# A two-layer graph network on one core: how the first layer forms and adds its messages' parts

## The chip, the core and the metric

The program runs on one of the eight cores of a Trainium2 chip. The metric is the device time of one execution in microseconds (us). The engines are named as in the profile: PE is TensorE (PEld is its weight load), DVE is VectorE, ACT is ScalarE, POOL is GpSimd and SP is SyncE.

## What is computed

There are 6250 nodes with 128 features and 100000 edges, sorted by their target `dst`. All is float32. The first layer is, with a layer norm behind it:

```python
msg_input = jnp.concatenate([h[src], h[dst], edge_feat], axis=-1)
messages = jax.nn.silu(msg_input @ W1 + b1) @ W2 + b2
agg = jax.ops.segment_sum(messages, dst, num_segments=h.shape[0])
upd_in = jnp.concatenate([h, agg], axis=-1)
h_new = jax.nn.silu(upd_in @ W3 + b3) @ W4 + b4
return h_new + h
```

The second layer sums `h[src]` by target, applies two small matrices, a layer norm and a relu. The change touches only the first layer.

## The kernel before

The edges stand in 196 groups of 512 (`GE`), four edges on each of 128 partitions (`CH` = 4). Two groups make a pair, so there are 98 pairs (`NPAIR`), and the targets of a group lie in a window of 64 nodes (`W`).

**The table of source terms.** `h @ W1[:128] + b1` is computed once for all nodes and stored in the tensor src_term. For each group POOL issues four indirect DMAs (line 873), each of which brings one row for each of 128 edges into `gath`, a ring of eight slots, so POOL may be four pairs ahead. The first two pairs (`FROM_X`) gather rows of x itself instead. A group's gather waits until the slot's last content, eight groups before, was used. Before, that is the counter `pre_ps`.

**The pair's work.** DVE makes the window's target one-hots in `terms_l` (line 1923), one pass of 64 partitions for each half of the pair, which also counts the edges of each node into `deg_col`. ACT copies the turned edge features and the window's target terms four times over (lines 1013 and 1014). In `pre_sums` PE multiplies them, four products of 128 rows a half (line 1233), adds the gathered rows by a product with the identity (line 1240), and counts `pre_ps` up. ACT applies silu into `msg` (line 1022). In `message_sums` PE sums messages by target with the one-hots `oh` (line 1250) and the degrees (line 1252). DVE adds these sums to `S` and `T` (`add_sums`, lines 1934 to 1938).

**The order.** Each engine runs turns (`steps`), and the list of stages at its end gives for each stage a lag: stage (lag, body) does pair s - lag in turn s. Each engine does the stages of a turn in the order of the list and waits in order. On DVE a turn is: unit rows of the node update (`rows0`, every second turn), `windows` of pair s-1, `one_hots` of s-2, `add_sums` of s-3, then `sort_edges`. `sort_edges` is a bitonic sort of the first half's edges by source, which the second layer uses; it fills turns 5 to 42 in portions. After turn 45 `early_hots` takes its place: one-hots for sums of the second layer that are made ahead. On PE a turn is `turn_ef` of s-1, `pre_sums` of s-2, `early_sums` and `early_rows`, `message_sums` of s-3, then the node update of a tile every second turn.

**After the pairs.** POOL issues 16 more gathers for two bridge blocks and then computes the last tile's inverse root (line 918). The rows of the first layer must all be stored before the second layer begins (line 1993 on DVE, line 1421 on PE).

## Time and profile before

| | us |
|---|---|
| median of the three runs | 1933.41 |
| lowest and highest run | 1929.03, 1937.31 |
| span of the profiled execution, first to last instruction | 1500.6 |
| its own time beside the span | not recorded; the timed median lies 432.8 above the span |
| busy of PE, PEld, DVE, ACT, POOL | 1285.9, 1063.6, 1014.5, 642.1, 1107.0 |

A row of a timeline is: start, duration, engine, line, operation, written<-read tiles, shapes, and in brackets how long the engine was idle before it and what ended that. DMA-issuing instructions are not counted as busy on other queues, and a matmul's duration overlaps the next one's, so that the pace of products is read from start to start.

### The profile page before, as it was taken

To read this page: it belongs to the slowest core of one execution; us is meant where nothing else is said; L and a number is where in the kernel's file an instruction comes from. 1 tells how busy PE (TensorE), PEld (TensorE's weight loads), DVE (VectorE), ACT (ScalarE), POOL (GpSimd) and SP (SyncE) were. 2 spreads that over 40 slices of the span, in tenths; PEclk is the share of its full clock that TensorE was granted. 3 is DMA by queue.
4 is the path that set the end of the run, shared out by engine and by line. 5 is a ranking of instruction groups with operands and counts; after the bars stand their busy time and mean duration, and the time that the engine had idled before them with its cause. 6 is when DMAs were issued, how large, how long until landed. Compare 5 with 4: busy or idle time off the path is not lost.

```text
span 1500.6 us, 31339 instructions
## 1 busy us (share of the span) xinstructions
PE 1285.9 (86%) x8165; PEld 1063.6 (71%) x8165; DVE 1014.5 (68%) x2310; ACT 642.1 (43%) x1257; POOL 1107.0 (74%) x1164
## 2 busy tenths in 40 slices
PE   6788789778777889888888888885999999999992
PEld 6666667556556667767767776764899999998982
DVE  4678888677665565665566656643666888878866
ACT  2744556555555555555556555551111111111111
POOL 5777777777777777777777777777777777777771
PEclk9898889999998999999999999997999999999996
DMA  6533333333336454454455445433887778778731
GB/s 206 135 85 92 93 95 94 95 96 91 95 90 119 118 138 125 126 136 131 125 131 133 125 128 135 113 80 105 258 261 230 208 230 241 222 230 241 213 92 47
DMA packets 189124, 214.15 MB, mean 143 GB/s; under 512 B 60426, under 2 KB 149517, under 8 KB 189011
## 3 DMA queue, kind: packets, MB, share of 16 engines
q1 hardware_dynamic: 138399, 131.62, 28.9%
q0 software_dynamic: 36352, 74.52, 21.3%
q10 hardware_dynamic: 14260, 6.68, 1.6%
q8 instruction: 49, 0.80, 0.2%
q14 instruction: 64, 0.52, 0.1%
HBM read 202.74 MB, written 9.85 MB: 142 GB/s over the span
## 4 chain that ended last, share of the span: by engine, by line
POOL 42%; PE 32%; issue 15%; DVE 4%; DMA 4%; SPq 1%; ACT 1%; DVEq 0%; ACTq 0%; POOLq 0%
POOL gath L873 42%; PE bank L1434 9%; PE bank L1410 8%; PE bank L1362 4%; DMA gath<-src_term,src_col 2%; PE bank L1240 2%; PE bank L1250 2%; PE bank L1233 2%; PE bank L1421 1%; DMA T<-in_x 1%; DMA gath<-layer_input,src_col 1%; PE bank L1396 1%; PE bank L1383 1%; PE bank L1441 0%; PE bank L1456 0%
## 5 line engine op out<-in xcount | busy, mean ns | idle before, releaser
L873 POOL DMA_INDIRECT gath<-src_term,src_col x768 | 737.2, 960 | 234.2 <-issue 230.2
L873 POOL DMA_INDIRECT gath<-layer_input,src_col x336 | 329.6, 981 | 105.6 <-issue 100.6
L1240 PE MATMUL bank<-gath,ident 128*128 128x512 f32 x384 | 218.3, 652 | 114.5 <-DMA gath<-src_term,src_col 113.8
L1233 PEld LDWEIGHTS bank<-terms_r,terms_l 128*128 128x128 f32 x1568 | 209.4, 201 | 83.1 <-issue 69.2
L1233 PE MATMUL bank<-terms_r,terms_l 128*128 128x128 f32 x1568 | 219.6, 286 | 30.4 <-ACT msg L1022 22.0
L1923 DVE TENSOR_SCALAR_CACHE_REDUCE terms_l<-dst_bc,node_col 64x512 f32<-64x512 int32 x196 | 221.0, 1128 | 13.1 <-issue 7.2
L1250 PEld LDWEIGHTS bank<-oh,msg 128*128 128x128 f32 x1568 | 198.7, 202 | 26.9 <-issue 26.1
L1934 DVE TENSOR_TENSOR S<-S,bank 128x128 f32 x98 | 28.1, 286 | 270.2 <-PE bank L1252 178.2
L1250 PE MATMUL bank<-oh,msg 128*128 128x128 f32 x1568 | 202.3, 285 | 0.0
L1434 PE MATMUL bank<-S 128*128 128x288 f32 x672 | 170.0, 406 | 0.1
L1649 DVE TENSOR_TENSOR oh<-bank,dst_rel 128x1024 f32<-128x1024 f32 x140 | 169.8, 1213 | 0.0
L1240 PEld LDWEIGHTS bank<-gath,ident 128*128 128x128 f32 x384 | 61.2, 201 | 129.7 <-DMA gath<-src_term,src_col 129.4
L1434 PEld LDWEIGHTS bank<-S 128*128 128x128 f32 x672 | 124.5, 190 | 31.1 <-issue 0.2
L1022 ACT ACTIVATE msg<-bank 128x512 f32<-128x512 f32 x196 | 115.8, 599 | 59.8 <-PE bank L1240 57.4
L1013 ACT COPY terms_l<-bank 64x512 f32<-64x512 f32 x196 | 113.7, 580 | 40.0 <-PE bank L1203 28.6
L1076 ACT COPY S<-bank 128x512 f32<-128x512 f32 x84 | 49.2, 586 | 185.8 <-PE bank L1410 181.8
L1993 DVE TENSOR_TENSOR S<-bank,dst_of 128x2304 f32<-128x2304 f32 x44 | 112.0, 2548 | 10.1 <-PE bank L1434 3.8
L1014 ACT COPY terms_r<-bank 64x512 f32<-64x512 f32 x196 | 113.4, 578 | 0.0
L1035 ACT ACT_TABLE_LOAD x48 | 61.6, 1283 | 66.9 <-DVE mv L2025 66.4
L1362 PE MATMUL bank<-oh,gath 128*128 128x128 f32 x672 | 84.4, 279 | 5.1 <-DMA gath<-layer_input,src_col 5.1
L1362 PEld LDWEIGHTS bank<-oh,gath 128*128 128x128 f32 x672 | 80.4, 195 | 5.7 <-DMA gath<-layer_input,src_col 5.7
L1987 DVE TENSOR_SCALAR xT<-xT,even_odd 128x1024 f32<-128x1024 f32 x84 | 60.5, 762 | 5.4 <-DMA xT<-sorted_src 5.4
(219 smaller groups left out, 1754.7 us busy)
## 6 DMA issues: line engine op xcount, KB each, us to landing
dst_bc<-in_dst SPq DMA_DIRECT2D x195, 128.0 KB
xT<-sorted_src SPq DMA_DIRECT2D x42, 512.0 KB
xs<-layer_input SPq DMA_DIRECT2D x136, 128.0 KB
gath<-src_term,src_col POOLq DMA_INDIRECT x768
terms_l<-layer_input SPq DMA_DIRECT2D x88, 128.0 KB
terms_r<-layer_input SPq DMA_DIRECT2D x88, 128.0 KB
msg<-layer_input SPq DMA_DIRECT2D x80, 128.0 KB
ef_s<-in_edge_attr SPq DMA_DIRECT2D x97, 64.0 KB
```

Source lines behind the costliest of these rows:

```text
L873: g.indirect_dma_start(out=to[:, j * D:(j + 1) * D], out_offset=None, in_=table[0:rows, :], in_offset=bass.IndirectOffsetOnAxis(ap=indices ...
L1013: a.copy(terms_l[r, u, h, :, :], bank[4][r, 0:P].unsqueeze(1).to_broadcast([W, CH, P]))
L1014: last = a.copy(terms_r[r, u, 1 - h, :, :], bank[4][r, P:2 * P].unsqueeze(1).to_broadcast([W, CH, P]))
L1022: a.activation(msg[:, 2 * (m % 2) + h, :], bank[h][:, :], ACT.Silu).then_inc(msg_made, 1)
L1233: mm(bank[h][:, j * D:(j + 1) * D], terms_l[:, u, h, j, :], terms_r[:, u, h, j, :], start=j == 0, stop=False)
L1240: mm(bank[h][:, :], ident[:, :], gath[:, slot, :], start=False, stop=True).then_inc(pre_ps, 1)
L1250: mm(bank[2 + u][:, 0:PW], msg[:, 2 * u + c // CH, c % CH * D:(c % CH + 1) * D], oh[:, u, c, :], start=c == 0, stop=c == 2 * CH - 1)
L1362: last = mm(bank[2 + u][:, 0:PW], gath[:, s, c % CH * D:(c % CH + 1) * D], oh[:, u, c, :], start=c == 0, stop=c == 2 * CH - 1)
L1410: last = mm(bank[h][:, c * D:(c + 1) * D], src_hot[:, u, w, e], x_near[m][h * CH + c][:, w, :], start=w == 0, stop=w == 1)
L1434: last = mm(bank[4][:, 0:DW], rows_kept[:, c // CH, c % CH * D:(c % CH + 1) * D], dst_hot[:, u, c, :], start=o % LATE == 0 and c == 0, sto ...
L1649: ve_.tensor_tensor(oh[:, u, :, :], iota_ps.unsqueeze(1).to_broadcast(shape), dst_rel[:, ds((k + first) * (2 * CH), 2 * CH)].unsqueeze(2). ...
L1923: ve_.tensor_scalar(terms_l[r, u, h, :, :], dst_bc[r, u, :].rearrange("n (p j) -> n j p", j=CH), node_col[r, ds(k, 1)], None, ALU.is_equal ...
```

## The change

The operands of the first layer's products are laid out anew, and the gathered rows are added elsewhere.

- `windows`: one DVE pass of 128 partitions makes both one-hots (`dst_is`), without counting. ACT counts in a new stage `degrees`, a copy of 128x512 with a sum.
- `edge_features`: one ACT copy of 128x256 to `ef_b` in place of four of 64x512. The edge weights `wef_of` are a constant.
- `pre_sums`: for each half one 64-row product of 512 columns, then four 64-row products of 128 columns each, the halves in turn. The identity product is gone. Half h of pair k waits for `rows_added` of half h of pair k-1, since both use bank h.
- `add_rows`: a new last stage of DVE's turn, pair s-2. It waits for PE's bank and for the gathered rows and writes their sum to `msg`. ACT's silu works on `msg` in place. The ring's slot is free once `rows_added` counts.

```diff
@@ load_pair (SP)
-                sp.wait_ge(ohT_made, done(2 * k - 3))
+                sp.wait_ge(ohT_made, done(k - 2))
@@ gather_sources (POOL)
                     if g >= RING:
-                        pool.wait_ge(pre_ps, done(g - RING))
+                        pool.wait_ge(rows_added, done(g - RING))
@@ edge_features, degrees, messages (ACT)
-                for h in range(2):
-                    r = slice(h * W, (h + 1) * W)
-                    a.copy(terms_l[r, u, h, :, :], bank[4][r, 0:P].unsqueeze(1).to_broadcast([W, CH, P]))
-                    last = a.copy(terms_r[r, u, 1 - h, :, :], bank[4][r, P:2 * P].unsqueeze(1).to_broadcast([W, CH, P]))
-                last.then_inc(efT_made, 1)
+                a.copy(ef_b[:, u, :], bank[4][:, 0:2 * P]).then_inc(efT_made, 1)
+
+            def degrees(k, m, q):
+                act.wait_ge(ohT_made, done(k))
+                act.wait_ge(sums_ps, done(k - DEEP))
+                act.wait_ge(deg_made, done(k - 1))
+                a.activation(pre[:, :].rearrange("p (j e) -> p j e", j=CH), dst_is[:, m % 2, :, :], ACT.Copy,
+                             accum_out=deg_col[:, m:m + 1]).then_inc(deg_made, 1)
...
-                    act.wait_ge(pre_ps, done(g))
-                    act.wait_ge(sums_ps, done(k - 2))
-                    a.activation(msg[:, 2 * (m % 2) + h, :], bank[h][:, :],
-                                 ACT.Silu).then_inc(msg_made, 1)
+                    act.wait_ge(rows_added, done(2 * k + h))
+                    of = msg[:, 2 * (m % 2) + h, :]
+                    a.activation(of, of, ACT.Silu).then_inc(msg_made, 1)
@@ pre_sums (PE)
+                for h in range(2):
+                    pe.wait_ge(rows_added, done(2 * k + h - 2))
+                    mm(bank[h][:, :], ef_b[own[h], u, 0:P], wef_of[own[h], :], start=True, stop=False)
+                for j in range(CH):
+                    for h in range(2):
+                        last = j == CH - 1 and not from_rows
+                        made = mm(bank[h][:, j * D:(j + 1) * D], dst_is[own[h], u, j, :], ef_b[own[h], u, P:2 * P],
+                                  start=False, stop=last)
+                        if last:
+                            made.then_inc(pre_ps, 1)
@@ windows, add_rows (DVE)
+                dve.wait_ge(deg_made, done(k - 2))
+                ve_.tensor_scalar(dst_is[:, u, :, :], dst_bc[:, u, :].rearrange("n (p j) -> n j p", j=CH),
+                                  node_col[:, ds(k, 1)], None, ALU.is_equal).then_inc(ohT_made, 1)
+
+            def add_rows(k, m, q):
+
+                u = m % 2
+                dve.wait_ge(sums_ps, done(k - 2))
                 for h in range(2):
...
+                    slot = 2 * m + h
+                    to = msg[:, 2 * u + h, :]
+                    dve.wait_ge(pre_ps, done(2 * k + h))
...
+                    dve.wait_ge(gathered[slot], 16 * CH * (q + 1))
+                    ve_.tensor_tensor(to, bank[h][:, :], gath[:, slot, :], ALU.add).then_inc(rows_added, 1)
@@ the stage lists (ACT, DVE)
-                  of_pair(1, edge_features), of_pair(0, window_x),
+                  of_pair(1, edge_features), of_pair(0, window_x), of_pair(2, degrees),
...
-                  of_early(1, early_hots))
+                  of_early(1, early_hots), of_pair(2, add_rows))
```

The order of DVE's instructions around the end of turn 5, before: from the sums' addition (`S`) past the last exchange of the sort portion to the next turn's windows. The sort portion between is left out.

```order
L1934 ISA [waits sums_added,sums_ps,zeroed]
L1934 TENSOR_TENSOR S<-S,bank 128x128
L1744 TENSOR_TENSOR src_rows_f<-src_rows_f,bank 112x64x2x2 [waits sort_steps]
L1923 TENSOR_SCALAR terms_l,deg_col<-dst_bc,node_col 64x512 [waits sums_ps,pre_ps,dst_bc_in1]
L1923 TENSOR_SCALAR terms_l,deg_col<-dst_bc,node_col 64x512
L1649 TENSOR_TENSOR oh<-bank,dst_rel 128x1024 [waits sums_ps]
```

The same place now. `dst_rows_f` and `src_rows_f` are the sort's keys.

```order
L1949 ISA [waits sums_added,sums_ps,zeroed]
L1949 TENSOR_TENSOR S<-S,bank 128x128
L1748 TENSOR_TENSOR src_rows_f<-src_rows_f,bank 112x32x2x4 [waits sort_steps]
L1940 TENSOR_TENSOR msg<-bank,gath 128x512 [waits gathered_0,pre_ps,sums_ps]
L1940 TENSOR_TENSOR msg<-bank,gath 128x512 [waits gathered_1,pre_ps]
L1925 TENSOR_SCALAR terms<-dst_bc,node_col 128x512 [waits deg_made,pre_ps,dst_bc_in0]
L1653 TENSOR_TENSOR oh<-bank,dst_rel 128x1024 [waits sums_ps]
```

The two additions into `msg` stand behind the sort portion and ahead of the next turn's windows, and wait for gathers, for PE and for the pair before the last.

PE's order for one pair before (from `pre_sums` of pair 3 to `message_sums` of pair 2).

```order
L1233 MATMUL bank<-terms_r,terms_l 128x128 [waits msg_made,ohT_made,efT_made]
L1233 MATMUL bank<-terms_r,terms_l 128x128 x3
L1240 MATMUL bank<-gath,ident 128x512 [waits gathered_6]
L1233 MATMUL bank<-terms_r,terms_l 128x128 [waits msg_made]
L1233 MATMUL bank<-terms_r,terms_l 128x128 x3
L1240 MATMUL bank<-gath,ident 128x512 [waits gathered_7]
L1250 MATMUL bank<-oh,msg 128x128 [waits msg_made,sums_added,oh_made]
L1250 MATMUL bank<-oh,msg 128x128 x3
L1250 MATMUL bank<-oh,msg 128x128 [waits msg_made]
L1250 MATMUL bank<-oh,msg 128x128 x3
```

And now, where `terms` holds `dst_is`, `ef_b` and `wef_of`.

```order
L1234 MATMUL bank<-terms 128x512 [waits rows_added,ohT_made,efT_made]
L1234 MATMUL bank<-terms 128x512 [waits rows_added]
L1238 MATMUL bank<-terms 128x128 x8
L1254 MATMUL bank<-oh,msg 128x128 [waits msg_made,sums_added,oh_made]
L1254 MATMUL bank<-oh,msg 128x128 x3
L1254 MATMUL bank<-oh,msg 128x128 [waits msg_made]
L1254 MATMUL bank<-oh,msg 128x128 x3
L1257 MATMUL bank<-ident,deg_col 1x128 [waits deg_made]
```

The waits for gathers left PE. In their place the second product of 512 columns waits for DVE's addition for the pair before, and the message sums of that pair still stand behind it.

## Rows read from the trace of the kernel before

**Rows 1.** The page: span, and the chain that ended last by engine.
```profile
span 1500.6 us, 31339 instructions
...
POOL 42%; PE 32%; issue 15%; DVE 4%; DMA 4%; SPq 1%; ACT 1%; DVEq 0%; ACTq 0%; POOLq 0%
```

**Rows 2.** POOL: the group of gathers, and its last work ahead of layer two.
```profile
L873 POOL DMA_INDIRECT gath<-src_term,src_col x768 | 737.2, 960 | 234.2 <-issue 230.2
...
1034.72 0.25 POOL L918 TENSOR_SCALAR var_eps<-mv 128x2 f32<-128x2 f32 x1
```

**Rows 3.** Windows: busy time by engine, PEclk (granted clock), DMA share, GB/s.
```profile
115.00:125.00 10.00, 6.61 (x30) 4.83 (x29) 7.57 (x25) 7.20 (x13) 7.63 (x8) 0.71 0.38 101
150.00:300.00 150.00, 122.38 (x722) 94.64 (x721) 117.86 (x297) 86.44 (x168) 113.95 (x119) 0.91 0.37 94
300.00:450.00 150.00, 118.02 (x691) 89.68 (x690) 103.78 (x256) 82.35 (x158) 113.77 (x119) 0.92 0.37 93
600.00:750.00 150.00, 132.56 (x858) 105.36 (x857) 92.67 (x215) 84.80 (x172) 114.02 (x119) 1.00 0.49 129
```

**Rows 4.** Timeline of DVE: end of turn 5, then turn 6.
```profile
90.32 0.42 DVE L1744 TENSOR_TENSOR src_rows_f<-src_rows_f,bank 112x256 f32<-112x256 f32 x1
94.14 0.27 DVE L1934 TENSOR_TENSOR S<-S,bank 128x128 f32 x1
...
94.81 0.41 DVE L1736 COPY bank<-src_rows_f 112x256 f32<-112x256 f32 x1
...
98.64 0.42 DVE L1744 TENSOR_TENSOR src_rows_f<-src_rows_f,bank 112x256 f32<-112x256 f32 x1
```

**Rows 5.** Timeline of PE after an idle stretch, and one pair later.
```profile
120.73 2.04 PE L1233 MATMUL bank<-terms_r,terms_l 128*128 128x128 f32 x8 [3.39 <-ACT msg L1022]
122.56 1.91 PE L1240 MATMUL bank<-gath,ident 128*128 128x512 f32 x2
...
125.98 1.07 PE L1240 MATMUL bank<-gath,ident 128*128 128x512 f32 x2
126.88 1.95 PE L1250 MATMUL bank<-oh,msg 128*128 128x128 f32 x16
128.76 0.38 PE L1252 MATMUL bank<-ident,deg_col 128*1 128x128 f32 x2
...
132.16 1.05 PE L1233 MATMUL bank<-terms_r,terms_l 128*128 128x128 f32 x8
133.05 1.02 PE L1240 MATMUL bank<-gath,ident 128*128 128x512 f32 x2
```

**Rows 6.** Groups of DVE instructions between 10 and 60 us, shapes kept apart.
```profile
L1545 DVE TENSOR_TENSOR T<-bank,b_bc 128x512 f32<-128x512 f32 x12 | 8.3, 688 | 12.9 <-PE bank L1160 7.6 <-DMA b_bc<-in_L_gnn_b 5.3
L1923 DVE TENSOR_SCALAR_CACHE_REDUCE terms_l<-dst_bc,node_col 64x512 f32<-64x512 int32 x5 | 5.6, 1130 | 2.3 <-issue 2.2
```

**Rows 7.** Timeline of a turn with early work of the second layer.
```profile
709.44 0.62 DVE L1987 TENSOR_SCALAR xTs<-As,even_odd 128x256 f32<-128x256 f32 x2
...
709.83 1.05 POOL L873 DMA_INDIRECT gath<-src_term,src_col  x1 [0.30 <-issue]
...
709.97 0.75 DVE L1993 TENSOR_TENSOR src_rows_f<-bank,dst_of 128x576 f32<-128x576 f32 x1
...
714.61 1.13 PE L1396 MATMUL bank<-dst_rows_f,As 128*128 128x288 f32 x4
...
715.58 1.05 PE L1383 MATMUL bank<-xs,xTs 128*128 128x128 f32 x8
```

**Rows 8.** Timeline of the first layer's end.
```profile
1016.11 1.29 PE L1240 MATMUL bank<-gath,ident 128*128 128x512 f32 x2 [3.17 <-DMA gath<-src_term,src_col]
...
1024.50 0.29 DVE L1934 TENSOR_TENSOR S<-S,bank 128x128 f32 x1 [2.60 <-PE bank L1252]
...
1031.98 0.25 DVE L2025 BATCH_NORM_AGGREGATE mv<-st 128x2 f32<-128x6 f32 x2
...
1039.10 5.02 DVE L1993 TENSOR_TENSOR S<-bank,dst_of 128x2304 f32<-128x2304 f32 x2 [2.67 <-DMA layer_input<-ot]
```

More of the change, by code:

```diff
@@ L897, in gather_bridge @@
                     g = 2 * k + h
-                    pool.wait_ge(pre_ps, done(g - RING))
+                    pool.wait_ge(rows_added, done(g - RING))
                     gather_rows(x1_d, EARLY_TILES * P, g % RING, bridge_rows[:, k - NPAIR, h * CH:(h + 1) * CH],
@@ L1110, in any_messages @@
                 act.wait_ge(any_pre_ps, done(i - 1))
[L1111 removed]
+                a.copy(ef_b[0:W, 0, 0:P], bank[4][0:W, 0:P]).then_inc(any_efT_made, 1)
                 act.wait_ge(any_pre_made, done(i))
@@ L1227, in pre_sums @@
                 pe.wait_ge(efT_made, done(k))
-                pe.wait_ge(ohT_made, done(2 * k + 1))
+                pe.wait_ge(ohT_made, done(k))
+                from_rows = isinstance(k, int) and k < FROM_X
+                own = [slice(h * W, (h + 1) * W) for h in range(2)]
                 for h in range(2):
-                    g = 2 * k + h
-                    pe.wait_ge(msg_made, done(g - 2))
-                    for j in range(CH):
-                        mm(bank[h][:, j * D:(j + 1) * D], terms_l[:, u, h, j, :], terms_r[:, u, h, j, :],
-                           start=j == 0, stop=False)
-                    if isinstance(k, int) and k < FROM_X:
-                        add_from_x(g, bank[h])
-                        continue
-                    slot = 2 * m + h
-                    pe.wait_ge(gathered[slot], 16 * CH * (q + 1))
-                    mm(bank[h][:, :], ident[:, :], gath[:, slot, :], start=False, stop=True).then_inc(pre_ps, 1)
+                    pe.wait_ge(rows_added, done(2 * k + h - 2))
[7 more added lines that the diff above has]
+                            made.then_inc(pre_ps, 1)
+                if from_rows:
+                    for h in range(2):
+                        add_from_x(2 * k + h, bank[h])
             def message_sums(k, m, q):
```

109 lines of the change are left out of this document (52 added, 57 removed).

## The prediction

> **What bounds the kernel now.** First the page: the chain that ended last gives 42% of the span to POOL and 15% to issue, which in the first layer is the gap between two gathers [rows 1]. The group of gathers says what a gather costs: 960 ns busy and 234.2/768 = 0.30 us idle, put down to issue and not to another engine [rows 2]. So one gather takes 1.26 us, the eight of a pair 10.1 us, and 98 pairs about 991 us. In the windows POOL is busy 114 of 150 us in every stage of the first layer, which is 119 gathers of 1.26: POOL never stops [rows 3]. PE, DVE and ACT are fitted under it. DVE is the next: 117.9 of 150 us between 150 and 300 us, where the sort runs, against 92.7 of 150 after it [rows 3]. At the end POOL counts once more: after the last pair's rows come 16 bridge gathers, and then the last inverse root at 1034.72; the second layer begins at 1039.10 [rows 2, 8]. From there PE is the bound, and the change does not touch that part.
>
> So what PE, DVE or ACT save inside the first layer is worth nothing as long as POOL is fed. What the change can do is to let the engines behind POOL fall back. The question is one turn of DVE: is it longer than 10.1 us?
>
> **The change part by part.** *DVE's own work.* Two passes of 1130 ns and their counts go [rows 6], 2.3 us. One pass of 128x512 comes, for which I have no row of the same form: it lies between the two-column-value pass of 128x256 (0.31 us each, two in 0.62 [rows 7]), doubled in size, 0.5 us, and the old pass, 1.13 us. I take 0.8 (either way it lies beside PE's work and is not on the path below). Two additions of 128x512 from PSUM come, priced at the 688 ns of the nearest form [rows 6], 1.3 us in start to start. In sum DVE does a little less than before.
>
> *ACT.* Four copies become one, and a counting copy comes. ACT was far from its limit, the counts have a turn's time until PE asks for them, so this is priced at nothing; if it were on the path it would cost one 0.6 us copy a pair.
>
> *PE.* Per pair two groups of identity products go, 0.86 us each from start to start (125.98 to 126.88 holds 0.90) [rows 5]. Two products of 512 columns come, with 64 rows, at the same price. Eight products of 128 columns stay, 0.89 us for four (132.16 to 133.05) [rows 5], now of 64 rows with the halves in turn. No row shows two halves of the array at work together: the bounds are 1.8 us a pair, as now, and half of it, 0.9. I take the middle, 1.35.
>
> *SP, POOL.* SP's loads wait for the same pass as before, POOL's gathers for `rows_added` eight groups back instead of `pre_ps`: nothing as long as the lag stays under some 28 us (three pairs less the landing).
>
> *The new ring of waits.* This is the cost. Call E(k) the time at which DVE ends the second addition of pair k. Behind it come, each waiting for the one before: PE's second 512-column product of pair k+1 (it needs bank 1), its small products, the message sums of pair k, DVE's addition of these sums, DVE's sort portion, and only then the additions of pair k+1, for DVE works in order and the additions stand last in its turn. Behind a waiting addition stand DVE's next windows, its one-hots and the next sort portion, and PE and ACT wait for these. Before, no addition stood there: DVE sorted while PE worked on the pair.
>
> At PE's higher clock the turn is: 1.1 (the rest of the first wide product, which started 0.65 us before E, and the second) + 1.35 small + 1.9 message sums (126.88 to 128.76) + 0.3 degrees + 0.2 until DVE starts [rows 5] = 4.8. Then 0.7 for the sums (94.14 to 94.81), the sort portion 4.2 (94.81 to 99.06; the portions of turns 6 to 19 are alike but for one of 3.2), and 1.3 for the additions [rows 4, 6]. Sum 11.0 us, with 10.6 and 11.5 for the two prices of the small products. That is already over 10.1.
>
> But then PE, with some 7 us of work a turn, is idle for about 4 us in each. What such an idle does is in the trace: after 3.39 us of idle the same four products take 1.8 us from start to start and not 0.89, and this lasts from 120.73 to 125.98, 5.3 us [rows 5]; the granted clock of that window is 0.71, a part at 1.2 GHz and the rest at 2.4 [rows 3]. So I reckon PE's part anew with the first 5.3 us at the lower level: wide products 1.7 each, of which E comes 0.65 into the first, so E+2.8; small ones 1.8 to 2.7, so E+4.6 to 5.5; sums and degrees at the higher level again, 2.2, and 0.2: E+7.0 to 7.9, middle 7.4. With 0.7, 4.2 and 1.3 the turn takes **13.6 us** (13.2 to 14.1). It leaves PE idle for some 4 us again, so it repeats itself.
>
> *The sum along E.* In the kernel before the sort portion of turn 5 ends at 90.74 [rows 4]. Now turn 5 ends with E(3), and turns 3 to 5 already wait for additions and for PE behind them: some 4 us more, and 1.3 for the additions themselves, E(3) = 96. Turns 6 to 19: 14 x 13.6 = 190. Turns 20 to 44 have portions from 0.4 to 5.4 us; DVE is busy 103.8 of 150 us there [rows 3], the long portions lose what the short ones win, and I take 25 x 10.2 = 255. Turns 45 to 93 carry the early work. There PE has 1.86 us more between the small products and the message sums (714.61 to 715.58, and 0.89 for the next eight instructions), DVE 1.3 in place of the sort (709.44 to 710.72) [rows 7]: 4.8 + 1.9 + 0.7 + 1.3 + 1.3 = 10.0, at the higher clock, since PE is idle under 2 us of it and PEclk is 1.00 in that stage already [rows 3]. 49 x 10.0 = 490. The last six turns have neither, 4.8 + 0.7 + 1.3 and unit rows, 7.8 each: 47. E(97) = 96 + 190 + 255 + 490 + 47 = 1078. Then 0.6 silu, half the message sums, degrees and DVE's start, 3.3 in all, and from the sums' addition to the second layer what it was, 1039.10 - 1024.50 = 14.6, less the 2.5 us for which DVE's mv at 1032.2 waited for POOL at 1034.72: 12.1 [rows 8, 2]. The second layer begins at 1078 + 3.3 + 12.1 = 1094 in place of 1039: **+55 us**, and the span is 1555. The profile's span is 1500.6, the median of the runs 1933.41, and I carry the 432.8 between them over unchanged: **1988 us**. This case's own range: with 13.2, 9.6 (small products overlapping) and a slower end bound by POOL +37, with 14.1 and 10.5 throughout +95, so 1970 to 2028.
>
> **Rules beside the rows.** Of overlapping halves no row here shows anything. The Trainium skill (TensorEngine Tiling (Array Packing), Tiling Modes) has two row tiles of 64 work in parallel, and a change of tiling mode drain the array. By the first the turns would take 13.2 and 9.6 us and the whole +37, by the second more than I took; the sum above goes by the middle.
>
> **The rivals.** *POOL still paces (0.17).* If PE's part behind E is shorter than I think, or the clock stays up with halves overlapping, the turn of 10.6 us falls back 0.5 us in each of 14, the ring takes it up, and it is regained in the short turns. Then POOL's 10.1 us a pair set the time, as its unbroken row says [rows 2, 3]: 1933, with at most 5 us either way. *The ring binds at the higher clock (0.19).* Turns of 11.0 to 11.5 us and E(3) = 96: E(17) = 96 + 157 = 253, 46 behind the gathers, of which 28 are free, so POOL is held up for 15 to 20 us: 1950. [...]
>
> *DVE's pass holds up the gathers (0.06).* The gather that runs beside the pair of passes at 709.44 takes 1.05 us and not 0.96 [rows 7]. If the new pass, a form without a count, does the same, each pair costs POOL 0.1 us, up to 0.3 for a pass of twice the length: 98 x 0.1 to 0.3 = 10 to 29 us, 1943 to 1962. The Trainium skill (GPSIMD Engine Reference, Specifications) says that GpSimd shares its SBUF interfaces with VectorE, which contend when VectorE is in a 2-port mode; by that rule, the trace agrees. Where DVE's ring already binds, this is hidden.
>
> *The other side: the last turns get shorter (0.05).* Message sums of pair 96 no longer stand behind the last pair's gather. From that landing at 1016.1 to 1024.5 there are 8.4 us [rows 8], now about 0.65 + 3.3: 4.4 less. POOL's inverse root caps that at 2.5 us unless it comes earlier; with PE kept at its higher clock into the second layer it could be some 9 to 10 us, 1923. This decides only if no turn is over 10.1 us.
>
> The forecast has 0.53. A measurement tells from no change what is over 0.5%, 9.7 us. Slower by more: 0.53 + 0.19 + 0.04 of the pass = 0.76; within: 0.17 + 0.02 = 0.19; faster: 0.05. The range goes from 1932, in the middle of the case in which POOL paces, to 2030.
>
> **What would show it.** Right: POOL's gathers waiting for DVE's L1940 from about 95 us on; DVE idle ahead of the sums' addition in each sort turn by some 4 us, released by PE's degrees product; PE idle ahead of its 512-column product, released by DVE's addition; PEclk between 0.7 and 0.85 from 100 to 250 us; a turn of 13 to 14 us there and 10 later; the second layer starting near 1094 and unchanged in length. Wrong: POOL busy 114 of 150 us throughout, small products at 0.45 us for eight instructions, or a sort turn under 10.5 us. The forecast errs most in the clock, which doubles PE's part, and in turns 45 to 93, where 0.5 us a turn is 25 us.

## The result, and the profile after

| us | before | after |
|---|---|---|
| median of four runs | 1931.72 | 2185.73 |
| lowest and highest | 1929.03, 1937.31 | 2179.06, 2188.75 |
| span of the profiled execution | 1500.6 | 2177.2 |

The changed kernel takes 1.1288 times as long, interval 1.1248 to 1.1328. That is 254 us more, where I had forecast 55. Its profiled execution took 2179.06 us, 1.9 more than its span, so here a trace shows the whole of what is timed. The page of the changed kernel, against [rows 1, 2]:

```profile
span 2177.2 us, 31275 instructions
...
PE 1402.9 (64%) x8173; PEld 1148.2 (53%) x8173; DVE 973.7 (45%) x2212; ACT 526.7 (24%) x1159; POOL 1104.5 (51%) x1161
...
L874 POOL DMA_INDIRECT gath<-src_term,src_col x768 | 741.0, 965 | 739.2 <-DVE msg L1940 514.9
...
L1949 DVE TENSOR_TENSOR S<-S,bank 128x128 f32 x98 | 28.3, 289 | 768.4 <-remote 416.6
...
L1925 DVE TENSOR_SCALAR terms<-dst_bc,node_col 128x512 f32<-128x512 int32 x98 | 66.9, 683 | 6.7 <-issue 6.7
```

A gather still takes 965 ns, but the idle time in front of the 768 has gone from 234.2 to 739.2 us, and 514.9 of it ends with DVE's addition (line 1940). DVE itself waits 768.4 us in front of its addition of the message sums (line 1949). DVE and ACT are less busy than in the profile of before, POOL as busy, and PE is 117 us busier (1402.9 against 1285.9) at a mean granted clock of 0.778 against 0.945. The rest of the added time is waits. Windows of the changed kernel, columns as in [rows 3]:

```profile
150.00:300.00 150.00, 70.99 (x407) 60.85 (x407) 69.57 (x194) 37.21 (x83) 69.17 (x72) 0.70 0.21 55
...
900.00:1050.00 150.00, 100.32 (x557) 73.49 (x558) 56.94 (x131) 43.59 (x103) 74.50 (x78) 0.73 0.32 86
1200.00:1350.00 150.00, 103.67 (x574) 76.23 (x572) 56.25 (x131) 44.60 (x101) 76.68 (x79) 0.73 0.34 87
```

72 gathers in 150 us are 16.7 us a pair, 79 are 15.2, against 10.1 before [rows 3]. PEclk is low in the last two stages as well, where I had put PE at its higher clock. The additions give E(k) as I called it. DVE's rows of the changed kernel at E(3) (the second of the two ends 0.6 us later), E(17), E(42), E(91) and E(97):

```profile
120.76 0.68 DVE L1940 TENSOR_TENSOR msg<-bank,gath 128x512 f32<-128x512 f32 x1
...
358.26 1.28 DVE L1940 TENSOR_TENSOR msg<-bank,gath 128x512 f32<-128x512 f32 x2
...
744.29 1.29 DVE L1940 TENSOR_TENSOR msg<-bank,gath 128x512 f32<-128x512 f32 x2
...
1486.18 1.27 DVE L1940 TENSOR_TENSOR msg<-bank,gath 128x512 f32<-128x512 f32 x2
...
1560.60 1.29 DVE L1940 TENSOR_TENSOR msg<-bank,gath 128x512 f32<-128x512 f32 x2
```

| step | forecast us | measured us |
|---|---|---|
| E(3) | 96 | 122.0 |
| turns 6 to 19 | 14 x 13.6 = 190 | 14 x 17.0 = 237.5 |
| turns 20 to 44 | 25 x 10.2 = 255 | 25 x 15.4 = 386.0 |
| turns 45 to 93 | 49 x 10.0 = 490 | 49 x 15.1 = 741.9 |
| last six | 47 | 74.4 |
| E(97) | 1078 | 1561.9 |
| E(97) to the second layer | 15.4 | 15.0 |

So every turn is some 3.4 to 5.2 us over my sum. But the kernel before has as much that its one profile did not show, and that has to come first.

### The profile page after: what moved, and what is told of

The parts are those of the page before. It is cut to its first block, busy times and chain, and to the rows that moved or that the text cites. A ratio compares the mean times of both kernels' runs of the same rounds, so it can differ in the third digit from the quotient of the medians.

```text
span 2177.2 us, 31275 instructions
## 1 busy us (share of the span) xinstructions
PE 1402.9 (64%) x8173; PEld 1148.2 (53%) x8173; DVE 973.7 (45%) x2212; ACT 526.7 (24%) x1159; POOL 1104.5 (51%) x1161
## 3 DMA queue, kind: packets, MB, share of 16 engines
HBM read 202.74 MB, written 9.85 MB: 98 GB/s over the span
## 4 chain that ended last, share of the span: by engine, by line
another core or an unknown queue 49%; issue 13%; DVE 12%; SPq 10%; PE 9%; DVEq 3%; ACT 2%; DMA 1%; ACTq 0%; POOLq 0%; POOL 0%
PE bank L1439 3%; DVEq L1944 2%; SPq L719 2%; SPq L781 2%; PE bank L1415 2%; SPq L784 2%; DVE msg L1940 1%; DVE bank L1740 1%; DVE src_rows_f L1744 1%; DVE oh L1653 1%; SPq L733 1%; SPq L792 1%; ACT S L1077 1%; DVE src_rows_f L1748 1%
## 5 line engine op out<-in xcount | busy, mean ns | idle before, releaser
L874 POOL DMA_INDIRECT gath<-src_term,src_col x768 | 741.0, 965 | 739.2 <-DVE msg L1940 514.9
L1234 PE MATMUL bank<-terms 64*128 64x512 f32 x392 | 225.0, 1120 | 344.3 <-DVE msg L1940 341.1
L1949 DVE TENSOR_TENSOR S<-S,bank 128x128 f32 x98 | 28.3, 289 | 768.4 <-remote 416.6
L1024 ACT ACTIVATE msg<-msg 128x512 f32<-128x512 f32 x196 | 122.0, 630 | 953.9 <-DVE msg L1940 925.8
L1234 PEld LDWEIGHTS bank<-terms 64*128 64x128 f32 x392 | 71.6, 305 | 367.8 <-issue 287.2
L1254 PE MATMUL bank<-oh,msg 128*128 128x128 f32 x1568 | 223.2, 289 | 56.0 <-issue 54.5
L1238 PEld LDWEIGHTS bank<-terms 64*128 64x128 f32 x1568 | 219.6, 315 | 61.9 <-issue 61.3
L1439 PE MATMUL bank<-S 128*128 128x288 f32 x672 | 192.9, 444 | 34.9 <-ACT S L1077 30.3
L1238 PE MATMUL bank<-terms 64*128 64x128 f32 x1568 | 198.3, 396 | 0.0
L1202 PE MATMUL bank<-ident,ef_s 128*128 128x128 f32 x98 | 37.5, 382 | 175.0 <-ACT As L1069 132.5
L1367 PE MATMUL bank<-oh,gath 128*128 128x128 f32 x672 | 103.4, 288 | 59.2 <-issue 58.0
L1940 DVE TENSOR_TENSOR msg<-bank,gath 128x512 f32<-128x512 f32 x192 | 122.9, 681 | 0.9 <-DVE dst_rows_f L1748 0.5
L1925 DVE TENSOR_SCALAR terms<-dst_bc,node_col 128x512 f32<-128x512 int32 x98 | 66.9, 683 | 6.7 <-issue 6.7
```

The source lines that it names most:

```text
L874: g.indirect_dma_start(out=to[:, j * D:(j + 1) * D], out_offset=None, in_=table[0:rows, :], in_offset=bass.IndirectOffsetOnAxis(ap=indices ...
L1024: a.activation(of, of, ACT.Silu).then_inc(msg_made, 1)
L1234: mm(bank[h][:, :], ef_b[own[h], u, 0:P], wef_of[own[h], :], start=True, stop=False)
L1238: made = mm(bank[h][:, j * D:(j + 1) * D], dst_is[own[h], u, j, :], ef_b[own[h], u, P:2 * P], start=False, stop=last)
L1254: mm(bank[2 + u][:, 0:PW], msg[:, 2 * u + c // CH, c % CH * D:(c % CH + 1) * D], oh[:, u, c, :], start=c == 0, stop=c == 2 * CH - 1)
L1367: last = mm(bank[2 + u][:, 0:PW], gath[:, s, c % CH * D:(c % CH + 1) * D], oh[:, u, c, :], start=c == 0, stop=c == 2 * CH - 1)
```

## The kernel before, profiled again

The kernel before without a change, once more.

> The kernel before, unchanged, once more. The profiled span of the kernel before was 1500.6 us while its timed executions took 1932, and that of the changed kernel was 2177 against 2186. Theory A (the one profiled execution of the kernel before was unlike its timed ones, and the timed ones wait longer after each semaphore): a profile of a span near 1925, POOL idle for more than 0.30 us ahead of many gathers, and an addition of the sums that starts 1 to 3 us after PE's degrees product. Theory B (430 us lie outside the span): span 1500 again, time 1932.

Measured: 1893.91 us against 1897.55 for the runs of before beside it, ratio 0.9985 (0.9953 to 1.0016). Its profiled execution took 1891.83 us with a span of 1889.9. So theory A came true, though DVE's addition starts later still than it said. The 432.8 us do not lie outside the span: the first profile was of an execution unlike the timed ones. Windows of its two layers, for the first profile (1500.6), this one and the changed kernel, in this order:

```profile
0.00:1039.10 1039.10, 858.62 (x5297) 678.93 (x5297) 666.13 (x1614) 568.23 (x1097) 777.45 (x828) 0.94 0.44 115
1039.10:1500.00 460.90, 427.23 (x2868) 384.68 (x2868) 348.38 (x696) 73.90 (x160) 329.57 (x336) 0.96 0.70 206
```
```profile
0.00:1297.80 1297.80, 975.21 (x5297) 750.27 (x5297) 669.87 (x1614) 561.61 (x1097) 776.33 (x828) 0.86 0.34 92
1297.80:1889.00 591.20, 472.43 (x2868) 408.27 (x2868) 349.72 (x696) 69.55 (x160) 326.37 (x336) 0.90 0.54 161
```
```profile
0.00:1576.90 1576.90, 929.74 (x5305) 739.66 (x5305) 623.12 (x1516) 457.07 (x999) 777.72 (x826) 0.73 0.29 75
1576.90:2177.00 600.10, 473.15 (x2868) 408.49 (x2868) 350.54 (x696) 69.61 (x160) 326.75 (x336) 0.91 0.55 159
```

The second layer takes 591 us as timed and 600 after the change: it is the same, as forecast. The first layer takes 1298 us and not 1039, so a pair took 12.5 us on average between the first gather and the last, and POOL, with the same 777 us of work, waited for a fifth of the time beyond its 0.3 us between gathers. By these two profiles the change adds 279 us to the first layer; up to 38 us of that are not the change, since before took 1931.72 us in the runs beside the changed kernel and 1893.91 here. Where the 259 us between the two profiles of before go is seen in one turn of this second profile (POOL's last gather of a turn, PE's degree product, DVE's addition of the sums that waits for it, SP, POOL's next gather):

```profile
799.35 0.38 PE L1252 MATMUL bank<-ident,deg_col 128*1 128x128 f32 x2
...
802.62 0.96 POOL L873 DMA_INDIRECT gath<-src_term,src_col  x1 [0.30 <-issue]
...
805.12 0.84 SPq L780 DMA_DIRECT2D xs<-layer_input  x2
805.45 0.29 DVE L1934 TENSOR_TENSOR S<-S,bank 128x128 f32 x1 [4.35 <-remote]
...
807.89 0.96 POOL L873 DMA_INDIRECT gath<-src_term,src_col  x1 [4.31 <-PE bank L1240]
```

PE's degree product is done at 799.73 by its record. DVE's addition starts at 805.45; in the first profile it mostly took 0.2 us. Not all of these 5.7 us are lost in the wait: DVE was at other work until 801.10, and by the records of its sequencer it loaded the addition's places into registers until 802.7, so that 2.7 us are left. ACT's activation of line 1031, SP's loads and PE's own products (a gap of 1.27 us inside line 1233) go on at 805.1 to 805.4 too. POOL's eighth gather ended at 803.58. One turn on, it ended at 817.70, and DVE, SP and PE went on at 819.25 to 819.51. I call this the **hold-up**: the other engines' waits end about 1.5 us after the last gather of the eight. POOL was four pairs ahead at that time, so nobody waited for the data. The hold-up is not only one of signals between engines. PE's stop inside line 1233 stands before products that wait for nothing; between 300 and 1000 us this profile has 42 such stops of over 0.3 us, the first profile none. SP took 0.6 to 0.7 us for each of several register instructions at 803 to 805 that take 0.02 to 0.2 us elsewhere. "Remote" in such a row can be no other core, since the program runs on one; I read it as a signal whose record the trace lacks.

## Experiments on the additions' place

**e1**: the additions ahead of DVE's addition of the sums. **e7**: between it and the sort's portion.

```diff
-  of_pair(3, add_sums), (0, NPAIR, sort_edges), of_early(1, early_hots), of_pair(2, add_rows))
+  of_pair(2, add_rows), of_pair(3, add_sums), (0, NPAIR, sort_edges), of_early(1, early_hots))   # e1
+  of_pair(3, add_sums), of_pair(2, add_rows), (0, NPAIR, sort_edges), of_early(1, early_hots))   # e7
```

> The changed kernel with DVE's additions of the gathered rows moved ahead of the addition of the sums and of the sort portion in a turn. Theory A (the ring of waits through DVE's turn is the cost: additions stand behind sort portion and sums): the turn is no longer additions, PE, sums, sort in sequence, so most of the 254 us comes back: 1900 to 1990. Theory B (the 64-row products or the slower waits are the cost, wherever the additions stand): 2130 to 2190.

> The changed kernel with DVE's two additions between its addition of the message sums and the sort's portion (or the early one-hots), not at the end of the turn. Theory A (the ring of my prediction: additions, TensorE's products, message sums, DVE's addition of the sums, sort or one-hots, additions): only the sort's portion (3 to 4 us a turn in turns 6 to 42) and the early one-hots (1.6 us in turns 45 to 93) leave the ring, so the time lies between 1994 us (additions ahead of both) and 2186 us, at 2010 to 2080 us. Rival: what costs is any wait of DVE in front of the additions behind the message sums, and the ring's length is not the point: 2150 us or more. Second rival: the addition of the message sums was never on the ring and the sort's portion is all of it: 1994 us, as with the additions ahead.

Measured: 1994.29 us, ratio 1.0556 (1.0494 to 1.0617), and 1995.63 us, 1.0545 (1.0508 to 1.0582). For e1 that is just above theory A's 1990; for e7 it is below theory A and meets its second rival's figure. More than half of the loss is that the additions stand behind the sort's portion and the early one-hots. The second rival, that the addition of the sums costs nothing there, is not shown by it, for the two are equal in sum only: e1 has 75 gathers between 150 and 300 us and 96 between 900 and 1050, e7 89 and 86.

**e2**: the changed kernel with the gathered rows added by PE's identity product again, silu from the bank, no `add_rows`. **e3**: the kernel before with nothing but that part of the change.

```diff
-    # DVE: add_rows at the end of the turn                            (e2; e3 adds it to before)
+    mm(bank[h][:, :], ident[:, :], gath[:, slot, :], start=False, stop=True).then_inc(pre_ps, 1)
```

> The changed kernel with one part undone: PE adds the gathered rows by the identity product again and ACT's silu reads the bank; one-pass one-hots, counts on ACT and 64-row products in both halves stay. Theory A (the additions on DVE are the whole cost): 1900 to 1950, no slower than the kernel before. Theory B (the 64-row products, or the counts on ACT, cost): clearly over 1950, up to 2186.

> The kernel before with one part of the change alone: DVE adds the gathered rows at the end of its turn; two passes with counts, four ACT copies and 128-row products stay. Theory A (the additions at the end of DVE's turn are the whole cost): as slow as the changed kernel or slower, since DVE's two passes are longer by 1.6 us a turn: 2180 to 2300. Theory B: near the kernel before, 1930 to 2000.

Measured: e2 1907.12 us, ratio 1.0068 (1.0049 to 1.0088); e3 2133.77 us, 1.1253 (1.1211 to 1.1296). e2 is as theory A said; e3 is below the 2180 us of its theory A, but far from theory B. The additions are nearly the whole change. The one-pass one-hots, ACT's counts and the 64-row products together cost 0.7% and save nothing, though DVE does 163 us less.

**e8**: each addition done twice. **e9**: the one-hot pass done twice, each with a wait between the two.

```diff
+    ve_.tensor_tensor(to, bank[h][:, :], gath[:, slot, :], ALU.add).then_inc(added_once, 1)
     ve_.tensor_tensor(to, bank[h][:, :], gath[:, slot, :], ALU.add).then_inc(rows_added, 1)
```

> The changed kernel with each of the two additions of pairs 2 to 97 done twice (into the same tile, the second one releases the readers). Theory A (the additions stand on the ring that sets every turn): 1.4 us more in each of 96 turns, +120 to +150 us over the changed kernel, 2300 to 2340 us. Rival (the turn is set by something beside them, POOL's gathers or TensorE at its low clock, and DVE has room): under +40 us.

> The changed kernel with DVE's one-hot pass of every pair done twice. Theory A (the pass stands in front of DVE's wait for the message sums, not on the ring): DVE's idle time in front of the sums' addition takes the 0.7 us, and the ratio to the kernel before stays within 0.01 of the changed kernel's 1.129. Rival (DVE as a whole sets the turn, or its pass holds up the gathers): 98 x 0.7 us, 65 to 70 us more, a ratio of 1.16 or above.

Measured: e8 2219.46 us, ratio 1.1746 (1.1708 to 1.1784), beside 1890.16 for before, so 87 us over the changed kernel and not the 120 to 150 of theory A, nor the 40 of its rival. e9 2185.07 us, 1.1260 (1.1191 to 1.1328): the pass costs nothing, as theory A said. What counts of the additions is thus a little more than one of the two.

**e11**: ACT's `keep_early` ahead of its silus. **e12**: e11 and e1 together.

```diff
-  of_pair(2, messages(0)), of_early(2, keep_early), of_pair(2, messages(1)))
+  of_early(2, keep_early), of_pair(2, messages(0)), of_pair(2, messages(1)))
```

> The changed kernel with ACT's copy of the early rows (keep_early) ahead of its two silus, not between them. With it between, TensorE's first transpose of a turn waits for that copy, which waits for the first silu, which waits for the first addition: in the trace without gathers TensorE starts 0.38 us after the second addition's end and needs 0.83 us before its wide products, that is 1.2 us of the ring in turns 45 to 93, and the wide products for the first group could run before the additions' end, some 0.5 us more. Theory A (that wait is the piece my chain missed): 1.2 to 1.9 us in 49 turns, 60 to 95 us less than the changed kernel, a ratio of 1.08 to 1.10. Rival (the stalls fill any room that is made, or TensorE waits at its second wide product instead): under 25 us, a ratio of 1.115 or above.

> The changed kernel with both moves: the additions ahead of DVE's addition of the sums, and the copy of the early rows ahead of the silus. With the first alone the ratio was 1.056 and a turn about 12.5 us, which is POOL's eight gathers (10.1 us), about 1.5 us until the engines that stood go on, and the first addition (0.7 us), after which POOL's next gather starts. Theory A (that is what sets the turn now): the second move gives nothing, 1.045 to 1.06. Rival (TensorE's wait for the copy still counts): 1.02 or under.

Measured: e11 2167.00 us, ratio 1.1172 (1.1111 to 1.1234), some 23 us less and not 60, as the rival said; e12 2013.72 us, 1.0406 (1.0347 to 1.0466), some 29 us better than e1's ratio and between theory A and its rival, nearer to theory A. PE's wait at the turn's head is real, but it accounts for only a tenth of the loss.

## Experiments on the gathers

**e4, e5**: the changed kernel and the kernel before, in which the gathers of pairs 2 to 95 are plain transfers of as many rows, so that the sums are of other rows. **e10**: the kernel before with this done to the second group of each pair only.

```diff
-    gather_rows(A_d, N, g % RING, src_col[:, g * CH:(g + 1) * CH], gathered[g % RING])
+    for j in range(CH):
+        nc.gpsimd.dma_start(gath[:, g % RING, j * D:(j + 1) * D], A_d[j * P:(j + 1) * P, :]) \
+            .then_inc(gathered[g % RING], 16)
```

> The changed kernel, in which the four gathers of a group in pairs 2 to 95 are four plain transfers of 128 rows each into the same tiles (fixed rows of the same table instead of the gathered ones, so the sums are of other rows). Theory A: what makes a turn longer than the sum of the ring's pieces are stalls of the other engines that end 1.4 to 1.6 us after POOL's last gather of a turn (in the unchanged kernel POOL's last gather ends at 803.58 and 817.70 and the stalled engines go on at 805.10 and 819.25); without gathers the ring stands with its pieces alone, some 11 to 12 us instead of 14 to 15, and the time is 1850 to 2000 us. Theory B: the stalls have nothing to do with the gathers: POOL was not what the turn waited for, and the time stays within 2% of the changed kernel, 2140 to 2200 us.

> The kernel before with the same plain transfers in place of the gathers of pairs 2 to 95. Theory A (stalls that go with the gathers): the turn falls from 12.2 us to TensorE's own work of some 9.5 to 10.5 us, and the time to 1650 to 1780 us, further below its own than the pace of POOL alone would give. Theory B: at most what POOL's waits gave, 1850 to 1900 us. The ratio of this run's partner (the changed kernel with plain transfers) to this one then says what the additions in the ring cost without the gathers.

> The kernel before, in which the second group of each pair is loaded by plain transfers of fixed rows and the first is still gathered. With all gathers it takes 1890 us, with none 1516 us. Theory A (the stalls go with the number of gathers, each holding the other engines up for its time): about half way, 1650 to 1750 us. Theory B (it is the long unbroken run of eight gathers whose work piles up): nearly all of it comes back, 1516 to 1600 us. Theory C (any gather at all in the turn is enough): 1800 us or more.

| | us | ratio to before with gathers |
|---|---|---|
| e5, before, no gathers | 1515.85 | 0.8013 (0.7987 to 0.8039) |
| e10, before, four in a row | 1571.54 | 0.8103 (0.8059 to 0.8147) |
| e4, changed, no gathers | 1831.08 | 0.9696 (0.9663 to 0.9728) |

The direction is theory A's for both kernels, and both times lie below its ranges; for e10 theory B came true. Without gathers the kernel before gives back 374 us, and with four gathers in a row nearly as much. The bytes are the same in e5. Not all of the 374 us is hold-up: the first layer ends at 923.7 in e5 and at 1039.1 in the first profile, which had all its gathers and no hold-up, so some 115 us are POOL's pace, which the plain transfers (0.55 us each) take away as well. The changed kernel falls to 1831 us, and the two are then 315 us apart. With DVE's line 1942 of e4 for E(k), its turns stand beside the forecast's:

| us | forecast | e4, no gathers | changed |
|---|---|---|---|
| E(3) | 96 | 97.1 | 122.0 |
| one turn of 6 to 19 | 13.6 | 12.9 | 17.0 |
| one turn of 20 to 44 | 10.2 | 10.5 | 15.4 |
| one turn of 45 to 93 | 10.0 | 12.6 | 15.1 |
| last six | 47 | 61.5 | 74.4 |
| E(97) | 1078 | 1219.9 | 1561.9 |

Up to E(42) the ring without gathers takes what I had forecast (540.7 and 541 us). Its turn later is my ring with one more piece, shown here by one of the shortest (PE and DVE of e4 between 904 and 916 us; the numbers of its lines are two higher):

```profile
904.69 0.48 PE L1204 MATMUL bank<-ident,ef_s 128*128 128x128 f32 x1 [2.74 <-ACT As L1071]
904.96 0.63 PE L1206 MATMUL bank<-wab,xw 128*128 128x128 f32 x2
905.52 2.08 PE L1236 MATMUL bank<-terms 64*128 64x512 f32 x4
907.39 1.21 PE L1240 MATMUL bank<-terms 64*128 64x128 f32 x16
908.53 1.24 PE L1403 MATMUL bank<-src_rows_f,As 128*128 128x288 f32 x4
...
912.38 0.38 PE L1259 MATMUL bank<-ident,deg_col 128*1 128x128 f32 x2
```
```profile
912.95 0.29 DVE L1951 TENSOR_TENSOR S<-S,bank 128x128 f32 x1 [6.91 <-PE bank L1259]
...
913.75 0.61 DVE L2004 TENSOR_SCALAR xTs<-As,even_odd 128x256 f32<-128x256 f32 x2
...
914.95 1.28 DVE L1942 TENSOR_TENSOR msg<-bank,gath 128x512 f32<-128x512 f32 x2
```

From E at 904.31 to E at 916.23 are 11.9 us, each piece released by the one before it. DVE starts 0.19 us after PE's degree product. In the turns of 13.3 to 13.5 us that are two of every four, the small products and the early work take 4.5 us at a granted clock of 0.64 (880.60 to 885.07), against 3.1 us at 0.95 here (907.39 to 910.50): that is the clock's part, 1.4 us in such a turn.

**e13, e15, e16**: POOL waits before each group until the group before has landed; for the kernel before, the changed one, and e2. **e17, e18**: the same wait two gathers later. **e14**: the kernel before with four iotas of POOL ahead of each group, 1.2 us in its trace, which makes the gap between two groups 1.6 us in place of 0.3.

```diff
+    pool.wait_ge(gathered[(g - 1) % RING], 16 * CH * ((g - 1) // RING + 1))     # e13, e15, e16
     if g >= RING:
         pool.wait_ge(pre_ps, done(g - RING))                                    # e15: rows_added
```

> The kernel before with all its gathers; from pair 2 on POOL waits, before the four gathers of a group, until those of the group before have landed. Theory A (what stalls the other engines is a row of more than four or five gathers under way, whose transfers pile up): the stalls go, and the turn is set by POOL with its waits, 2 x (5.05 + 1.5 to 2.5 us) = 13 to 15 us at worst, or by TensorE if the wait is shorter than that; 1600 to 1900 us, below the unchanged kernel. Theory B (each gather costs its stall wherever it stands): the wait of POOL adds to the turn, 1950 us or more.

> The kernel before with all its gathers and a pause of POOL, four small iotas of about 0.2 us each, ahead of each group from pair 2 on, some 1 us a group and 2 us a pair. Theory A (transfers pile up in a row of eight): a pause lets them drain in part, 1650 to 1850 us. Theory B: no gain, 1880 to 1990 us.

> The changed kernel with the same wait of POOL for the landing of the group before. Without gathers its turn was 11.9 to 13.1 us (1831 us), the ring alone, with them 14 to 15. Theory A (stalls of piled transfers stand on top of the ring): 1850 to 2050 us. Theory B: no gain, 2130 to 2200 us. In either case it should stay over the kernel before with the same wait, by the ring.

> The changed kernel with the rows added by TensorE's identity product again (ratio 1.007 to before as it stood) and POOL's wait for the landing of the group before. Theory A: within 3% of the kernel before with that wait, on the slower side, since its product part takes TensorE 76 us more. Rival: DVE's 163 us and ACT's 100 us less of work let it be the fastest of all, 2% or more below.

> The kernel before with POOL's wait for the landing of the group before put between the second and the third gather of a group. The landing came 1.7 us after the last gather's end in the run with the wait ahead of the group, and two gathers take 2.5 us, so POOL hardly stops, while at most six gathers are under way. Theory A (the number under way is what holds up the others): the stalls go, 1550 to 1750 us. Theory B (it takes a pause of POOL): within 1.5% of the kernel before as it is, 1870 to 1930 us.

> The changed kernel with the same wait between the second and the third gather. Theory A: 1850 to 2000 us, as without gathers (1831 us) up to the run with the wait ahead of the group (2004 us). Theory B (the pause did it): within 2% of the changed kernel, a ratio of 1.11 to 1.15 to the kernel before.

| | without | with the wait ahead of the group | two gathers later |
|---|---|---|---|
| before | 1 | 1.0471 (1.0434 to 1.0509) | 1.0002 (0.9980 to 1.0025) |
| changed | 1.1288 | 1.0531 (1.0492 to 1.0570) | 1.1294 (1.1252 to 1.1337) |
| e2 | 1.0068 | 1.0528 (1.0497 to 1.0560) | not run |

e14 has 1.0098 (1.0071 to 1.0124). e15 and e16 came out as theory A said; e13, e14, e17 and e18 as theory B said. A wait that only makes POOL slower, with a pause of 1.8 us after every fourth gather, makes the changed kernel 7% faster: 2003.69 us. In its turn DVE's wait ends 0.2 us after PE's product, though gathers go on beside it; that is the usual case in e13, e14 and e15 alike, and PE has no stop of over 0.3 us before a product that waits for nothing there (300 to 1000 us):

```profile
907.27 0.38 PE L1258 MATMUL bank<-ident,deg_col 128*1 128x128 f32 x2
...
907.85 0.29 DVE L1950 TENSOR_TENSOR S<-S,bank 128x128 f32 x1 [2.84 <-PE bank L1258]
```

With the pauses POOL needs 13.7 to 13.9 us a pair, and that hides the ring: all three kernels are then within 0.6% of each other. For the kernel before it costs more than the hold-up did. In e14 the shorter pause ends the hold-up too, but POOL's pace is then 12.8 us a pair, against 12.5 with the hold-up. The limit on the number under way (e17, e18) changes nothing; it takes the pause. No version that gathers all its rows beats the kernel before; of those with a part of the change, e2 comes nearest.

## Why the forecast was wrong

**The ring: right.** POOL waits for line 1940 (514.9 us), DVE ahead of the sums' addition, PE ahead of its 512-column product for DVE's addition. e3 and e1 show that the additions at the end of DVE's turn do this by themselves, and in e4 the ring alone has turns of 12.9 and 10.5 us up to turn 44, where I had 13.6 and 10.2. That E(42) comes out within 1 us is partly luck, since the two errors cancel. PEclk is 0.70 from 100 to 250 us in the changed kernel, as forecast.

**The failed step: "POOL never stops", and "I carry the 432.8 between them over unchanged".** Both are from one execution. In the timed ones the kernel before has no pace of 10.1 us a pair behind which 4 us of a turn could vanish, and the 432.8 us are no fixed addition: by the second profile 259 of them are hold-ups and waits inside the first layer, to which the change adds. From e4 to the changed kernel E(97) goes from 1219.9 to 1561.9: these 342 us come with the gathers, and my sum had none of them.

**The term that was mis-sized: "4.8 + 1.9 + 0.7 + 1.3 + 1.3 = 10.0, at the higher clock".** Even without the hold-up (e4) it is 12.6 on average and 11.9 in the turn shown, 128 us over 49 turns. PE's first products do not start at the additions but behind ACT's copy of the early rows, which stands behind the first silu, and then behind the transpose and the window's product: 1.2 us until the wide products, and 1.9 for these, which fall into PE's lower clock level, 3.1 in place of 1.1. The other pieces came out as priced: small products 1.14 (1.35), early work 1.97 (1.86), sums and degrees with DVE's start 2.45 (2.4), additions of the sums, hots and rows 3.28 (3.3). "PE is idle under 2 us" was wrong by that copy: it is idle 2.7 to 3.6, and PEclk was 0.80 in that stage of e4 and 0.73 in the changed kernel, not 1.00.

**The missing ring: "POOL ... priced at nothing as long as the lag stays under some 28 us".** In the changed kernel POOL waits for the additions with all eight slots full, and the others' waits end when its eight gathers are through. The turn that was 11.9 us in e4 (POOL's first and last gather of a turn, DVE, POOL's next, in the changed kernel):

```profile
999.77 1.04 POOL L874 DMA_INDIRECT gath<-src_term,src_col  x1 [5.33 <-DVE msg L1940]
...
1008.67 0.95 POOL L874 DMA_INDIRECT gath<-src_term,src_col  x1 [0.30 <-issue]
...
1014.62 0.95 POOL L874 DMA_INDIRECT gath<-src_term,src_col  x1 [5.00 <-DVE msg L1940]
```
```profile
1008.54 0.38 PE L1257 MATMUL bank<-ident,deg_col 128*1 128x128 f32 x2
```
```profile
1011.67 0.29 DVE L1949 TENSOR_TENSOR S<-S,bank 128x128 f32 x1 [9.85 <-remote]
...
1012.47 0.62 DVE L2002 TENSOR_SCALAR xTs<-As,even_odd 128x256 f32<-128x256 f32 x2
...
1013.67 1.28 DVE L1940 TENSOR_TENSOR msg<-bank,gath 128x512 f32<-128x512 f32 x2
```

PE was done at 1008.92, DVE starts 2.75 us later, 2.05 after the last gather's end at 1009.62. In most turns of this stage it is PE that stands, inside the message sums, before products that wait for nothing. One turn on:

```profile
1023.42 0.95 POOL L874 DMA_INDIRECT gath<-src_term,src_col  x1 [0.31 <-issue]
1024.64 0.27 PE L1254 MATMUL bank<-oh,msg 128*128 128x128 f32 x1 [0.49 <-issue]
...
1026.06 0.51 PE L1254 MATMUL bank<-oh,msg 128*128 128x128 f32 x3 [1.16 <-issue]
...
1027.08 0.29 DVE L1949 TENSOR_TENSOR S<-S,bank 128x128 f32 x1 [5.83 <-PE bank L1257]
```

Either way DVE starts late after the last gather: 2.7 us here, 2.6 in the middle of the 23 turns between 900 and 1250 us. The turn at 999.77 adds up as: eight gathers 9.85, hold-up 2.05, sums and hots 2.00, the first addition and POOL's start 0.95, in all 14.85. In the sort's turns DVE waits at its place long before PE is done, and the hold-up is longest after PE's product, 5.5 us here:

```profile
364.96 0.38 PE L1257 MATMUL bank<-ident,deg_col 128*1 128x128 f32 x2
...
368.12 0.95 POOL L874 DMA_INDIRECT gath<-src_term,src_col  x1 [0.30 <-issue]
370.86 0.29 DVE L1949 TENSOR_TENSOR S<-S,bank 128x128 f32 x1 [9.60 <-remote]
```

There the portion of 4.2 us takes the place of 1.2, and with a hold-up of 1.8 (DVE at 370.86 after a last gather's end at 369.07) that is 17.6; 17.0 were measured over turns of which one has a shorter portion. By this sum a second first addition costs 0.74 us a turn, 71 us in 96 turns (e8: 87, not 130), the copy ahead of the silus nearly nothing (e11: 23), and a pass before DVE's wait nothing (e9). e7's turn also follows it:

```profile
1005.36 0.96 POOL L874 DMA_INDIRECT gath<-src_term,src_col  x1 [4.76 <-DVE msg L1940]
...
1014.24 0.96 POOL L874 DMA_INDIRECT gath<-src_term,src_col  x1 [0.30 <-issue]
1019.42 0.96 POOL L874 DMA_INDIRECT gath<-src_term,src_col  x1 [4.22 <-DVE msg L1940]
```

That is 9.84 for the gathers, 2.50 until DVE's sums at 1017.70, and 1.72 until POOL's next.

**The rivals.** That POOL's pace hides the ring came true only where POOL was made slower (e13, e15). DVE's pass beside the gathers does lengthen them, but at no cost in time: the mean gather took 960 ns before, 965 changed and 981 in e9, where 118 of the 162 gathers beside the second pass took over 1.0 us, and e9 was no slower. The new pass is 683 ns, between my bounds of 0.5 and 1.13. On the halves of the array e2 has rows at both clock levels, 1.00 in the first three and 0.50 in the last three:

```profile
901.40 1.13 PE L1235 MATMUL bank<-terms 64*128 64x512 f32 x4
902.37 1.06 PE L1238 MATMUL bank<-terms 64*128 64x128 f32 x16
903.35 1.12 PE L1244 MATMUL bank<-gath,ident 128*128 128x512 f32 x2
```
```profile
349.88 2.08 PE L1235 MATMUL bank<-terms 64*128 64x512 f32 x4
351.75 1.92 PE L1238 MATMUL bank<-terms 64*128 64x128 f32 x16
353.59 0.98 PE L1244 MATMUL bank<-gath,ident 128*128 128x512 f32 x1
```

From start to start the two wide products of 64 rows take 0.97 us and the sixteen instructions of the small ones 0.98, or 1.87 and 1.84 at the lower level. One wide product of 128 rows takes 0.9 [rows 5] and 1.7 by my own reckoning, and sixteen small instructions of 128 rows 1.78 and 3.6. So the two halves work together on both kinds, and my prices of 0.9 and 1.7 for each wide product were twice what it costs; the 1.51 us of the small products at 1003.18 in the changed kernel and the 1.14 in e4 are mixtures of the two levels. The Trainium skill (TensorEngine Tiling (Array Packing), Tiling Modes) has two row tiles of 64 work in parallel; by that rule 0.89 us would be reached for the small ones, and the trace agrees to 0.1 us. It saves nothing in e2, where the wide products came on top of the identity's: PE is 76 us busier there than in the second profile of before.

**What stays open** is what holds the engines up. It needs gathers, more than four in a row; it ends 1.5 to 2 us after the last one; a pause of 1.6 us (e14) or 1.8 us (e13, e15) between fours prevents it, one that leaves POOL's row unbroken does not. The DMA engines are not full at the time (their share in the first layer is 0.34). Late signals alone cannot be it, since products and register instructions that wait for nothing stand as well; no run here shows whether it is the supply of instructions or something else. Nor is it shown why one execution in the profile of before ran free of it, with its second layer 130 us shorter too. The clock's part in the loss was read only in e4's turns, not measured by an experiment.

## What to carry to other kernels

Before a forecast is built on a trace, hold its span against the timed runs: a gap of 29% meant here that the trace was of another regime, and then every "never stops" in it is to be doubted, and slack behind the busiest engine is not to be spent. Where an operation moves to an engine that works in order, its place in that engine's turn costs more than its duration: 1.3 us of additions cost some 240 us at the end of the turn (e3) and, with the rest of the change, some 100 ahead of the sort's portion (e1, e7). And a chain is followed through every engine that stands behind the moved result, with its queue: here the copy on ACT and the ring of slots on POOL were both released by the additions.

## What the runs showed of the hardware

- Eight indirect gathers in a row (1.26 us each) held up the other engines, waiting or not, until 1.5 to 2.7 us after the last: DVE, waiting already, until 5.5 us after PE's product (370.86 in the changed kernel), PE by up to 1.9 us before a product that waits for nothing (751.5 in the second profile of before). Four in a row hardly did (e10), and eight with a pause of 1.6 us or more between the fours did not (e13 to e15). Plain transfers of the same bytes took POOL 0.55 us each and the kernel 20% less time.
- The same program ran once in 1500.6 us of span and otherwise in about 1890 to 1940, with the same busy time of POOL (1107 and 1103 us).
- A slower POOL made a kernel faster: pauses of 1.8 us, 2186 to about 2004 us (0.933 by the two ratios).
- Products of 64 rows issued in turn to the two halves of the array (e2): two of 512 columns took 0.97 us at a granted clock of 1.00 and 1.87 at 0.50, sixteen instructions of 128 columns 0.98 and 1.84. Of 128 rows, one product of 512 columns takes 0.9 and sixteen such instructions 1.78 at 1.00.
- Gathers beside a DVE pass over 128x512 took over 1.0 us in 118 of 162 cases (e9); without any DVE work beside them they took 954 ns.
